# A graph network and a mixture of experts in one kernel: new order in the last stage, for the gate products, the state's products and the early fillings

## What is computed

```
x = x + gnn(layernorm(x), adj)
x = x + moe(layernorm(x))

def gnn(x, mask):                      # x: 16 x 512 x 128
    h = relu(bn(conv1(x)))             # 1 tap
    x_conv = relu(bn(conv2(h)) + x)    # 17 taps along the nodes
    s = x @ w_se.T + b_se              # 3 columns
    A = exp(-|s_i - s_j|^2) * mask
    x_nmp = A @ relu(x @ w_msg.T + b_msg)
    gi = concat(x_conv, x_nmp) @ w_ih.T + b_ih
    gh = x @ w_hh.T + b_hh
    r, z = sigmoid(gi_r + gh_r), sigmoid(gi_z + gh_z)
    return (1 - z) * tanh(gi_n + r * gh_n) + z * x

def moe(x):
    xn = layernorm(x) * gamma + beta
    w_full = softmax of the two highest of (xn @ Wr + br), 0 elsewhere   # 8 experts
    return sum_e w_full[e] * (gelu(xn @ W1[e] + b1[e]) @ W2[e] + b2[e])
```

## Time and profile before

| what | us |
|---|---|
| median of 3 runs | 616.95 (615.32 to 617.89) |
| the profiled execution, its own time | 613.4 |
| its span (first to last instruction) | 611.6 |
| PE busy | 587.0 |
| the chain that ended last | POOL's scatter-adds (L1034) from 581.4 on |
| mean time of one such add on POOL | 1.55 |
| store of `w_all`, issue to landing | 9.7 |

### The profile page before, as it was taken

The page is one execution under the profiler, slowest core; times in us unless marked ns, Lnnn a source line. Parts: engine busy times, 40 slices in busy tenths (PEclk is TensorE's granted clock), DMA queues, the critical chain, the costliest instruction groups (busy, mean ns, idle before and its releaser), DMA issues. The chain is left out here.

```text
span 611.6 us, 12890 instructions
## 1 busy us (share of the span) xinstructions
PE 587.0 (96%) x3936; PEld 515.5 (84%) x3936; DVE 478.4 (78%) x2014; ACT 366.6 (60%) x733; POOL 339.5 (56%) x249
## 2 busy tenths in 40 slices
PE   8999999999999999999999999999999999999991
PEld 6887778786879797979898989898898979999890
DVE  7978888898788988898989797979787966644330
ACT  5644637365858484848485767666675745655540
POOL 2000505133367577777776767778686563555765
PEclk9999999999999999999999999999999999999996
DMA  8519171725466757566666656657556778666853
GB/s 298 200 65 331 48 258 57 241 66 177 122 191 145 194 128 207 127 177 156 173 163 155 159 162 157 182 140 187 146 153 148 214 163 239 139 154 134 224 96 43
DMA packets 85861, 99.72 MB, mean 163 GB/s; under 512 B 7521, under 2 KB 62561, under 8 KB 85473
## 3 DMA queue, kind: packets, MB, share of 16 engines
q1 hardware_dynamic: 64064, 82.37, 43.3%
q0 software_dynamic: 21728, 16.53, 16.8%
HBM read 74.95 MB, written 30.39 MB: 172 GB/s over the span
## 5 line engine op out<-in xcount | busy, mean ns | idle before, releaser
L1013 POOL DMA_INDIRECT out<-y_t,xt x88 | 160.4, 1823 | 85.4 <-DMA out<-y_t,xt 53.0
L1048 POOL DMA_INDIRECT routed<-row,at_u x112 | 116.9, 1043 | 140.4 <-DVE at_u L1255 109.0
L570 PE MATMUL C<-cv_h,w_hi 128*128 128x256 f32 (+1 forms) x432 | 129.1, 299 | 3.3 <-ACT tz L926 1.5
L571 PE MATMUL C<-cv_l,w_hi 128*128 128x256 f32 (+1 forms) x432 | 123.4, 286 | 0.0
L572 PE MATMUL C<-cv_h,w_lo 128*128 128x256 f32 (+1 forms) x432 | 123.3, 286 | 0.0
L570 PEld LDWEIGHTS C<-cv_h,w_hi 128*128 128x128 f32 x432 | 81.7, 189 | 7.2 <-issue 3.2
L571 PEld LDWEIGHTS C<-cv_l,w_hi 128*128 128x128 f32 x432 | 81.5, 189 | 0.9
L572 PEld LDWEIGHTS C<-cv_h,w_lo 128*128 128x128 f32 x432 | 81.5, 189 | 0.7
L749 PE MATMUL G<-ex,msg_t 128*128 128x512 f32 x128 | 58.2, 597 | 1.7 <-ACT gh L945 1.7
L651 PE MATMUL Y<-w_t,ge 128*128 128x128 f32 x424 | 55.8, 274 | 0.0
L651 PEld LDWEIGHTS Y<-w_t,ge 128*128 128x128 f32 x424 | 51.7, 191 | 3.1 <-issue 2.6
(11 more groups left out here) (273 smaller groups left out, 1614.3 us busy)
## 6 DMA issues: line engine op xcount, KB each, us to landing
w_t<-w_all SPq DMA_DIRECT2D x63, 392.0 KB, 3.6
adj<-adj_t SPq DMA_DIRECT2D x16, 1024.0 KB, 5.8
xt<-routed SPq DMA_DIRECT2D x63, 144.0 KB, 2.4
wd<-w_all SPq DMA_DIRECT2D x11, 392.0 KB, 5.2
x_ln<-x SPq DMA_DIRECT2D x16, 256.0 KB, 2.8
x_res<-x_t SPq DMA_DIRECT2D x16, 256.0 KB, 6.0
out<-x SPq DMA_DIRECT2D x15, 256.0 KB, 3.9
w_all<-w_s SPq DMA_DIRECT2D x1, 3136.0 KB, 9.7
```

Source lines behind the costliest of these rows:

```text
L570: pe.matmul(psum, hi(w), rhs_h, start=start, stop=False)
L571: pe.matmul(psum, hi(w), rhs_l, start=False, stop=False)
L1013: nc.gpsimd.indirect_dma_start(out=out, out_offset=bass.IndirectOffsetOnAxis(ap=xt[j][:, t, R_ID:R_ID + 1].bitcast(U32), axis=0), in_=y_t[ ...
L1048: nc.gpsimd.indirect_dma_start(out=routed, out_offset=bass.IndirectOffsetOnAxis(ap=ats_u[d % 2][:, n:n + 1], axis=0), in_=rows[d % 2][:, n ...
```

## The change

1. `last_items`: tiles and dense items alternate from the start, T0 D T1 D ... T18 D, and the other 13 dense items follow. `loads_in_order` is changed with it; the second and third dense loads come behind the loads of T0 and T1. `SPACED` and `FRONT` fall away.
2. Before the last loads: the fillings of pad rows come first and wait only for `t_pad`, which DVE now makes right behind the counts in graph 14; then one dense load; then the wait for the tables.
3. PE: `conv_sum` does all nine taps, and `states` follows it. In routed graphs (d < 14) the n gate's product (`product_hn`) comes ahead of the z and r ones.
4. PE: the 16 bias products are spread over graphs 1 and 2, two at each of four places. DVE adds the bias in graph 3, and SP stores `w_all` in graph 3. The two large fillings move to graphs 1 and 2.
5. DVE: the sum `tr + C2` comes ahead of the half sum with `x_res`.

```diff
--- before.py
+++ after.py
@@ -44,7 +44,6 @@
 TILES = ROUTED * NODES * TOP // TILE + EXPERTS - 1
 STREAMED = SLOTS * (GRAPHS - FIRST)
 LAST = TILES - STREAMED
-SPACED = 4
 
 
 
@@ -53,7 +52,6 @@
 
 
 EARLY = 3
-FRONT = 4
 DENSE_LOADS = ([(e, (0,)) for e in range(EARLY)] + [(e, (0, 1)) for e in range(EARLY, EXPERTS)] +
                [(e, (1,)) for e in range(EARLY)])
 TAKEN = SLOTS * TILE
@@ -392,19 +390,14 @@
 
             dense = [(q, e, u, k) for k, (e, graphs) in enumerate(DENSE_LOADS) for q in graphs
                      for u in range(NODES // TILE)]
-            m, n, k = STREAMED, STREAMED, FRONT
-            for entry in dense[:k]:
+            m = STREAMED
+            for n, entry in zip(range(STREAMED, STREAMED + LAST), dense):
+                yield m, n, n % RING, 16 * (n // RING + 1)
+                yield m + 1, *entry
+                m += 2
+            for entry in dense[LAST:]:
                 yield m, *entry
                 m += 1
-            while n < STREAMED + LAST or k < len(dense):
-                if n < STREAMED + LAST:
-                    yield m, n, n % RING, 16 * (n // RING + 1)
-                    m, n = m + 1, n + 1
-                if n > STREAMED + SPACED or n == STREAMED + LAST:
-
-                    for entry in dense[k:k + 1 + n % 2]:
-                        yield m, *entry
-                        m, k = m + 1, k + 1
 
         items = list(last_items())
 
@@ -424,9 +417,11 @@
 
         def loads_in_order():
 
-            at = [(last_of_load(k - DENSE_BUFFERS), 1, k) for k in range(DENSE_BUFFERS, len(DENSE_LOADS))]
-            at += [(number.get(n - AHEAD, STREAMED), 0, n) for n in range(STREAMED, STREAMED + LAST)]
-            return [entry[1:] for entry in sorted(at)]
+
+            at = [(last_of_load(k - DENSE_BUFFERS), TILES, 1, k) for k in range(DENSE_BUFFERS, len(DENSE_LOADS))]
+            at += [(STREAMED, STREAMED + k - 1, 1, k) for k in range(1, DENSE_BUFFERS)]
+            at += [(number.get(n - AHEAD, STREAMED), n, 0, n) for n in range(STREAMED, STREAMED + LAST)]
+            return [entry[2:] for entry in sorted(at)]
 
         def run(iteration):
             for g in range(GRAPHS):
@@ -485,7 +480,7 @@
                         sp.wait_ge(added, 16 * TT * (n - RING + 1))
                     tile_loads(slot, *chosen[j])
 
-                if g == 1:
+                if g == 3:
                     sp.wait_ge(w12_ready, 2)
                     sp.wait_ge(w2_loaded, 16)
                     sp.wait_ge(b1_set, 1)
@@ -519,21 +514,21 @@
                         sp.wait_ge(rows_out[i], 16 * NT * TOP * ((g - i) // 2))
                     for j in range(2):
                         batch_load(g + 1, j)
+                if g == 1:
+                    sp.dma_start(routed[DUMMY + TAKEN:, :], pads[TAKEN:, :]).then_inc(pads_stored, 16)
                 if g == 2:
-                    sp.dma_start(routed[DUMMY + TAKEN:, :], pads[TAKEN:, :]).then_inc(pads_stored, 16)
-                if g == 3:
                     sp.dma_start(out[TOKENS + TAKEN:, :], pads[TAKEN:, 0:P]).then_inc(pads_stored, 16)
 
             chosen = []
             run(iteration)
 
 
-            for k in range(DENSE_BUFFERS):
-                dense_loads(k)
-            sp.wait_ge(tab_step, TAB_STEPS * (ROUTED - 1 - TAB_FIRST) + LAST_STEPS)
+            sp.wait_ge(tab_step, TAB_STEPS * (ROUTED - 1 - TAB_FIRST) + 2)
             for e in range(EXPERTS):
                 at = sp.value_load(t_pad[0:1, e:e + 1], min_val=e * REGION, max_val=e * REGION + TOKENS)
                 sp.dma_start(routed[bass.ds(at, TILE), :], pads[0:TILE, :]).then_inc(pads_stored, 16)
+            dense_loads(0)
+            sp.wait_ge(tab_step, TAB_STEPS * (ROUTED - 1 - TAB_FIRST) + LAST_STEPS)
             for i in range(2):
                 sp.wait_ge(rows_out[i], 16 * NT * TOP * ((ROUTED + 1 - i) // 2))
             sp.wait_ge(pads_stored, 16 * (EXPERTS + 3))
@@ -685,24 +680,30 @@
                 if is_graph(g, 1):
                     pe.wait_ge(wr_set, 2)
                     pe.wait_ge(w1_loaded, 16)
-                    for n in range(16):
-                        last = pe.matmul(H0[:, n:n + 1], w1_raw[:, n * P:(n + 1) * P], vec[:, V_BETA:V_BETA + 1],
-                                         start=True, stop=True)
-                    last.then_inc(pe_b1, 1)
+
+                def bias_products(first):
+
+                    if is_graph(g, 1) or is_graph(g, 2):
+                        for n in range(first + 2 * (g - 1), first + 2 * g):
+                            last = pe.matmul(H0[:, n:n + 1], w1_raw[:, n * P:(n + 1) * P], vec[:, V_BETA:V_BETA + 1],
+                                             start=True, stop=True)
+                        last.then_inc(pe_b1, 1)
+
                 tile_a(0)
+                bias_products(0)
                 if is_graph(g, 0):
                     pe.wait_ge(w_lo_done["conv_s"], 1)
                     pe.wait_ge(w_lo_done["conv_a"], 1)
                 pe.wait_ge(odd_split, g + 1)
                 if tail:
                     pe.wait_ge(gate_step, 2 * d + 2)
-                conv_sum(0, 5)
+                conv_sum(0, TAPS_A)
                 if tail:
                     pe.wait_ge(x1T_ready, d + 1)
                     pe.wait_ge(s_f32, g + 1)
                     states(STATES)
-                conv_sum(5, TAPS_A)
                 tile_b(0)
+                bias_products(4)
                 pe.wait_ge(msg_f32, g + 1)
                 pe.wait_ge(xlT_f32, g + 1)
                 transposes(M, msg_f).then_inc(pe_msgT, 1)
@@ -713,8 +714,6 @@
                 conv_diff(0, 4)
                 if is_graph(g, 0):
                     pe.wait_ge(rows_set, 1)
-                if is_graph(g, 1):
-                    pe.wait_ge(b1_set, 1)
                 pe.wait_ge(uv_split, g + 1)
                 dist(0)
                 if tail:
@@ -726,6 +725,7 @@
                 tile_a(1)
                 conv_diff(4, 14)
                 tile_b(1)
+                bias_products(8)
                 conv_diff(14, TAPS)
                 if tail and d >= ROUTED:
                     pe.wait_ge(xn_ready, d + 1)
@@ -734,11 +734,17 @@
                 if is_graph(g, 0):
                     pe.wait_ge(w_lo_done["gates"], 1)
                 pe.wait_ge(exp_done, NT * g + NT)
+                def product_hn():
+                    product(G0[:], HH + 2, xlT_h[:], xlT_l[:]).then_inc(pe_hn, 1)
+
+                if d < ROUTED:
+                    product_hn()
                 product(G1[:], HH + 1, xlT_h[:], xlT_l[:], stop=False)
                 product(G2[:], HH, xlT_h[:], xlT_l[:], stop=False)
-                if tail and d >= ROUTED:
+                if d >= ROUTED:
                     pe.wait_ge(xnT_f32, d - ROUTED + 1)
-                product(G0[:], HH + 2, xlT_h[:], xlT_l[:]).then_inc(pe_hn, 1)
+                    product_hn()
+                bias_products(12)
                 if more:
                     pe.wait_ge(xl_ready, g + 2)
                     transposes(M, flat(xl)).then_inc(pe_xT, 1)
@@ -1274,18 +1280,18 @@
 
                 def count():
                     step(nc.vector.tensor_scalar(t_c[:], COUNTS[0:1, :], float(TILE - 1) if every else 0.0, None,
-                                                 ALU.add), wait=False)
+                                                 ALU.add), wait=every)
+                    if every:
+                        step(nc.vector.tensor_scalar(t_pad[:], t_c[:], -float(TILE - 1), None, ALU.add), wait=False)
 
                 def tables(beside):
 
-                    done[0] = 1
-                    dve.wait_ge(tab_step, first + 1)
+                    done[0] = 2 if every else 1
+                    dve.wait_ge(tab_step, first + done[0])
                     s_e = [1, tiles, EXPERTS]
                     s_e1 = [1, tiles, EXPERTS + 1]
                     steps = cst[0:1, C_STEP:C_STEP + tiles]
                     oh, ends = t_oh[:, 0:tiles, :], t_le[:, 0:tiles, :]
-                    if every:
-                        step(nc.vector.tensor_scalar(t_pad[:], t_c[:], -float(TILE - 1), None, ALU.add), wait=False)
                     step(nc.vector.tensor_scalar(t_q[:], t_c[:], -TILE, None, ALU.bitwise_and), beside=beside)
                     step(nc.vector.tensor_tensor(t_a[:], t_q[:], t_d[:], ALU.subtract), beside=beside)
                     step(nc.vector.tensor_tensor(t_tri[:], cst[0:1, C_TRI8:C_TRI8 + 64].rearrange(
@@ -1421,7 +1427,8 @@
                         out=w_s[:, :, 2 * P:4 * P], in0=w1_raw[:].rearrange("p (e h) -> p e h", e=EXPERTS),
                         scalar=vec[:, V_GAMMA:V_GAMMA + 1], in1=w_s[:, :, 0:2 * P].bitcast(F32), op0=ALU.mult,
                         op1=ALU.subtract).then_inc(w12_ready, 1)
-                    dve.wait_ge(pe_b1, 1)
+                if is_graph(g, 3):
+                    dve.wait_ge(pe_b1, 8)
                     nc.vector.tensor_tensor(w_s[:, :, X_B1:X_B1 + HALVES].bitcast(F32),
```

(8 more changed lines are left out.)

## The result

The changed kernel took 627.11 us in the median of its four first runs (624.48 to 627.41), the kernel before 617.42 beside it (615.32 to 619.82): a ratio of 1.0141, 95% interval 1.011 to 1.0173. (Ratios and intervals here are estimated from all runs of a kernel and are not quite the quotients of the medians.) Forecast were 613.1 us and a range of 608 to 618. The prediction is wrong by 14 us and by its sign.

The account below looks back on a forecast made before the run. PE, busy 96%, bounds the kernel, with POOL ending last in the last stage today. Graph gains 2.5 + 2.3 + 0.5 - 1.0 = 4.3 us against +0.5 in the last stage give -3.8, from 616.95 to 613.1 us; range 608 to 618.

Parts of the forecast that it names:

- the cost of zero for moving the store of `w_all`: SP queue: storing `w_all` in graph 3 delays loads behind it, but no PE wait goes back to these; cost 0.
- the head start of 4.7 us for POOL: Last stage: T0's result is ready early, so POOL starts its tile adds 4.7 us sooner and ends 4.7 us sooner.
- Parts 2 and 3: Gate products, hn first: 2.5 us gained at waits for `gh`; DVE's sum before half sum: 2.3 in graphs 2 to 5.
- Part 4: Graphs 1 to 3: bias products in eight pieces gain 0.5 us, between -0.8 and +2; moved store and fillings cost 0.
- Part 5: Ten full graphs: state's products behind all nine taps use up 0.54 us cover, costing 0.1 each, 1.0 (0 to 3.0).
- rival (d): Full graphs: copies land later, ACT follows late; at 0.8 us lost each, +3.2 in all, 620.2 us; chance 0.04.
- Part 1: Last stage, alternating tiles and dense items: POOL ends sooner, PE waits for tiles and ends last; net +0.5 us.
- The total of PE's waits for `xt`: Last stage: PE waits some 8 us in all for tile loads, spread over T13, T15 and T17.
- The sign that the prediction named for it: Last stage: T0's first add comes some 4.7 us nearer to tile 43's last add.
- rival (c): Last stage: fillings or late T0 hold POOL, T0's add no sooner, stage 4.7 worse; +0.9, 617.9 us; chance 0.08.
- The 3.5 us of closing work: End of kernel: 3.5 us of closing work follow SP's last wait, added behind PE's end and the last store.
- Rival (e): Last stage: clock falls in PE's new waits, sign below 1.00 before PE's end; +2.4 us, 619.3; chance 0.04.

Follow-up runs that it names:

- the first measurement: Changed kernel, first timed beside the kernel before, its chip not on record: 627.11 us, ratio 1.0141.
- the first control: Changed kernel, nothing altered, timed a second time: 615.23 us, ratio 1.0004 to the kernel before.
- part 4 undone: Changed kernel with bias products in one block in graph 1, `w_all` stored in graph 1, two large fillings in graphs 2 and 3: 614.54 us, ratio 0.9989.
- The marks: Changed kernel with three tiny ScalarE copies, one behind each wait ahead of its state copies: 619.49 us without ratio; timed again 620.15 us, ratio 1.0112.
- the second control: Changed kernel, nothing altered, timed a third time: 614.99 us, ratio 1.0012 to the kernel before.
- parts 2 and 3 alone: Kernel before with hn's product first and DVE's sum `tr + C2` ahead of the half sum: 621.86 us, ratio 1.0084; timed again 611.69 us, 0.9941.
- the third set: Four kernels on one chip. Kernel before: early hn product and sum, 1.0084; new last-stage order, 1.0031; same, late fillings, 1.0006. Changed kernel: `w_all` store behind loads, 1.0142.

## Why the prediction was wrong

Three steps of the prediction failed: the cost of zero for moving the store of `w_all` (it costs PE 2.65 us), the head start of 4.7 us for POOL (it was 0.4 to 1.5), and, in the first measurement alone, late signals of PE, which no term of the sum held and whose origin stays open.

**Without the ACT waits**, the change is worth nothing (1.0004 and 1.0012, +0.2 and +0.7 us), where -3.8 us was forecast. By its terms:

- **Parts 2 and 3** (forecast 2.5 and 2.3, together -4.8): the pair alone measured 0.9941, that is 0.0059 x 615.0 = -3.6 us (2.2 to 5.0, so the forecast lies within). The mechanism is right. The wait for `gh` is gone, and the traces place the gain: the first tanh comes 1.3 us sooner (38.68 against 39.99), the graphs 2 to 5 are 0.7, 0.7, 0.7 and 0.2 us shorter. Graph 1 (30.5 against 29.2) is not comparable, since its clock fell behind the block there and not in the kernel before.
- **Part 4** (forecast -0.5, "cost 0" for the stores): this step failed. Graph 1 gains 2.0 us (27.6 against 29.6 with the block), graph 2 gives back 1.2 (27.3 against 26.1), and graph 3 pays 2.65 for `x_ln` behind `w_all` (28.8 against 26.1; in the first control 30.1, with the clock at 0.72 behind the waits). "No wait of PE goes back to these today" was read from a trace in which the store stood where it hurt nobody. With part 4 undone the kernel is at 0.9989 instead of 1.0004 to 1.0012: +0.9 to +1.4 us, a difference between sets that the intervals don't part from nothing; the 2.65 us are in the trace of both controls.
- **Part 5** (forecast +1.0): alone 1.0004, +0.2; a full graph takes 31.95 against 31.91 us, with 0.04 x 10 = 0.4. The marks show that the cover is used up, as reckoned: 0.3 us more on ACT costs 0.3 a graph. That is where rival (d) begins.
- **Part 1** (forecast +0.5): alone 1.0031, that is +1.9 us (0.5 to 3.3). From the tanh of graph 15 to the end of the span the last stage takes 112.9 and 114.0 us in the two controls, against 111.2; over all profiles, 112.4 to 115.5 in the thirteen with the order and the early fillings, 110.2 to 111.4 in the six with the old order. The total of PE's waits for `xt` came as forecast: 7.8, 7.5 and 7.8 us in the three profiles of the changed kernel, against some 8. The head start of POOL did not: 4.7 us became 0.4 to 1.5 us in the two controls, 1.0 alone, since tile 43's adds came 3.0 and 3.6 us later, counted from the tanh of graph 15. The sign that the prediction named for it, T0's add nearer to tile 43's, did come (2.6 and 3.2 us behind its end, where it was 7.1), because both had moved. That is rival (c), whose price of 4.7 was too large and whose chance of 0.08 too small. POOL's series from T0 to T11 was slower too, 58.5 and 59.7 us instead of 57.6, so PE could turn T17 only 75.0 and 77.3 us behind the tanh, not at the forecast 71.5, and ended at 109.4 and 110.1, not 104.9.

That the stage still comes out only 1.2 and 2.3 us above its forecast is luck, for a second error has the other sign. The 3.5 us of closing work were added behind the last store. They belong to POOL: its closing instruction lasts 13.54 us and outlasts the last add, to 611.3 in the kernel before; in the first control it is over at 610.5, before the store lands at 613.1, and the span ends 0.4 us behind that.

```profile
L170 POOLq DRAIN  x1: 13540/13540/13540, 597.8 to 597.8; - x1
L168 POOLq DRAIN  x1: 13537/13537/13537, 597.0 to 597.0; - x1
```

**The clock in the last stage.** Rival (e), with a chance of 0.04, named a sign, a clock below 1.00 before PE's end, and it came. Two windows of the first control, and the stage in the kernel before:

```profile
504.50:507.50 3.00, 3.00 (x16) 3.00 (x15) 0.75 (x4) 1.94 (x5) 1.55 (x1) 0.50 0.93 233
576.20:579.20 3.00, 3.00 (x16) 3.00 (x15) 1.37 (x6) 1.11 (x3) 2.66 (x2) 0.50 0.93 214
500.00:596.00 96.00, 93.78 (x806) 92.47 (x806) 47.37 (x207) 52.40 (x129) 56.32 (x37) 1.00 0.72 167
```

The first stands behind 2.43 us of idle of PE, for T0's split (2.42 at 516.01 above; PE stood 1.14 us for `y_t` at the start of the old order), the second behind 2.05 us for `xt` of T17. All fourteen profiles with the new order have one to three such stretches, none of the six with the old order has any before PE's end. 3 us at half the clock are 1.5 us of work lost (an estimate); the first is mostly taken up by the later waits for `xt`, the second is not. The wait for the split itself was in the sum, which let T0 begin at 503.4.

The measured parts add to -3.6 + 1.9 + 0.2 + (0.9 to 1.4) = -0.6 to -0.1 us, against +0.2 and +0.7 measured for the whole. One bound of the prediction does not follow from its own parts: the least gain in the graphs is 1.7 + 1.3 - 0.8 - 3.0 = -0.8, not 0.

**The further 12 us of the first measurement** are ACT's waits and what hangs on them: the graphs 2 to 4 took 3.0, 3.8 and 5.4 us longer than in the second control, 12.2 in all; PE's three waits are 10.2 of them, less the 1.2 that stood there anyway, and the rest is the lower clock behind, less the waits for `x_ln`, which they cover (0.23 us of PE in graph 3 instead of 2.65). The Trainium skill (TensorE: Matmul & The Clock Gate, "Why this matters for your kernels") warns of long idle between bursts: the trace agrees, with products of 0.42 us at 106.70 behind 4.14 us of idle. In the last stage the lower clock came behind shorter idle as well, 2.43 and 2.05 us. No rival had the cause of these waits.

What is shown of the cause: PE's signals come late, and that belongs to a set or its chip, not to the kernel. The changed kernel had it in one of three measurements, parts 2 and 3 alone in one of two. Late signals are in all five profiles of the first measurement and the third set, and in none of the other fifteen (there none is more than 0.3 us late). Its size hangs on the kernel: up to 4.85 us in the three that have parts 2 and 3, up to 0.9 us in the two without. Since the signals of the convolution and of the transposes are as late as that of the state's products, the store of the output rows and the router are not what was waited for, and ACT went on at once when the signal came. What stays open: what holds PE's signals, whether POOL's scatters have to do with it, why these parts make it large, and why one chip shows it and others don't. The kernels meant to tell this ran on chips where the control had no waits.

## What to carry over

A cost of zero for a moved store has to be checked against what will stand behind it in the same queue, not against who waits there today. A series that starts early gains only if everything ahead of it is early too: find the item that releases it and ask what that one waits for. And before a difference of one per cent is explained, run the same build again on another chip: four agreeing runs and a trace with the lost time in plain sight held for that one measurement only. And where a view names no releaser, look whether the signal itself came late.

## What the runs showed of the hardware

- PE's signals can come up to 4.85 us behind the recorded end of their matmuls (105.01, 105.10 and 105.16 for ends of 100.20, 101.12 and 102.17), and ACT then stands 3.5 to 3.8 us for them. All profiles of two measurements have late signals, the fifteen others have none.
- In or behind the block of 16 products of one column PE's clock fell to half (0.50: 1.2 of 2.4 GHz) in seven of ten profiles although PE was never idle (6.00 busy of 6.00 us); with the products in pieces of two, graph 1 took 27.6 us each time.
- Behind waits of 2.43 and 2.05 us in an otherwise busy stretch the granted clock was 0.50 for the next 3 us; behind waits of 2.15 and 2.16 us of the same stage it was not.
- A load of 256 KB issued 7.5 us behind a store of 3136 KB in the same queue needed 7.0 us to land instead of 2.9.
- POOL's closing instruction ends 5.0 us behind the end of its last scatter-add (606.37 to 611.3), so the end of a kernel can hang on POOL although all its adds have landed (SP's wait for them ends at 608.1).
